# A two-layer transformer on one core: two conditioning loads moved to ScalarE's queue, and the cosine's angle put behind the first tile's scaling

## The chip, the cores and the metric

The kernel runs on one core of a Trainium2 chip. A core has five engines that run their own instruction streams and meet only at semaphores: TensorE (PE, matmuls and transposes), VectorE (DVE), ScalarE (ACT), GpSimd (POOL) and SyncE (SP, which here only issues transfers). Transfers between HBM and the on-chip memory are issued by SP's queue and ACT's queue and are carried by 16 DMA engines. The metric is the device time of one execution in microseconds (us). The kernel before takes 905.02 us, the median of 3 runs (904.16 to 906.2).

## The reference, cut to what matters

Two layers are applied to x (2048 tokens of 512 features, 32 sequences of 64), both conditioned on one vector per sequence. What matters here is the start of the first:

```python
def ada_rms(x, t, w, tw):
    n = x * jax.lax.rsqrt(jnp.mean(jnp.square(x), axis=-1, keepdims=True) + EPS)
    scale = t @ tw.T                                   # the conditioning
    return n * (w * (1.0 + scale))[:, None, :]
def apply_rope(x, pos_ids):
    ang = pos_ids.astype(jnp.float32)[:, :, None] * inv_freq
    cos, sin = ...                                     # of ang, twice beside each other
    x1, x2 = (x[..., :half], x[..., half:])
    return x * cos + jnp.concatenate([-x2, x1], axis=-1) * sin
h = ada_rms(x, time_emb, ln1_w, ln1_tw)                # layer 0
q, k, v = h @ Wq.T, h @ Wk.T, h @ Wv.T                 # 8 query heads, 1 key/value head of 64
q, k = apply_rope(q, pos_ids), apply_rope(k, pos_ids)
attn = softmax(q k^T / 8);  x = x + (attn v) @ Wo.T
h = ada_rms(x, time_emb, ln2_w, ln2_tw)
x = x + (silu(h @ Wg.T) * (h @ Wu.T)) @ Wd.T           # 2048 inner features
```

The second layer (a layernorm with scale and shift from the same conditioning vector, 16 query heads of 32, masked attention, an output projection, no MLP) follows; it lies far behind the change.

## The kernel before

The 2048 tokens are 16 tiles (t = 0 to 15) of 128 tokens, two sequences each. Layer 0's attention goes tile by tile in a loop over s (from -1 to 15), layer 1's in a loop over u. The MLP works on blocks of 512 tokens in 16 groups of 128 inner features and is cut into pieces; two tables (FILL0, FILL1) say how many pieces each engine does at which place of the loops. The first pieces come at s = 5. Large products are done as three fp32r matmuls of high and low parts, so every operand has a "high" cast on ACT and a "low" subtraction on DVE or POOL. The order of work on each engine is written out by hand, and every engine executes its stream strictly in that order; dependencies are semaphores.

The change lies before the loops. What happens there, by engine:

- **SP** issues `condt` (the conditioning vectors, transposed), then four slices of 256 KB of `ln1_twT` into `adaw0` (L261, k = 0 to 3), `xt` of tile 0 (L241), four slices of the joined query, key and value weights into `wst` (L264), `xres` and `xt` of the next tiles, and larger weights.
- **ACT** issues `posi` (the positions), `invt` (the inverse frequencies), `idn` (the identity for transposes) and the two halves of `lnw`; then it loads its table for the sine, copies the conditioning product out of PSUM (`condition_copy`), makes the rotary tables (`rope_tables`: four Sin activations into `cs0`, behind one wait on `ang_ready`), and then does the high casts of the weights (`split_qkv(0)` to `(3)`), the squares of tiles 0 and 1 and the high cast of tile 1 (`high_h(1)`).
- **PE** runs `keep_warm(4)` (matmuls whose result nobody reads), four `condition(k)` (the product of `condt` with slice k, each behind its own semaphore `ld_ln1[k]`) with a `keep_warm(1)` between, the transpose of the result, `keep_warm(3)`, and `first_qkv()` (tile 0 times the weights, in plain fp32, behind `a_hf`). Then come three warming matmuls, the conditioning of the second norm, two more warming matmuls, and the transposes of tile 0's rotated queries and keys (`qk_T(0)`, L557).
- **DVE** waits for `posi` and `invt`, and works the rotary angles: position times frequency, reduced to within pi (L922 to L943, result in `ex`), and pi/2 minus its absolute value (L947, L950, result in `t1`, the cosine's angle), whose last instruction signals `ang_ready`. Then `adaptive_scale(0)` (L957) makes the scale table, `scale_h(0)` (L998) applies it to tile 0 and signals `a_hf`; then `split_qkv(0)`, `scale_h(1)`, `mean_sq(0)`, `split_qkv(1)` and `(2)`, and `rope_mul(0)` (L1012 to L1014), which needs the tables.

`split_qkv(k)` on DVE waits for ACT's cast of the same slice, and `high_h(1)` on ACT waits for DVE's `scale_h(1)`, so the two engines pass work back and forth from `split_qkv(0)` until `rope_mul(0)`. `rope_mul(0)` is followed by the sum on POOL (L343, L344), `qk_T(0)` on PE, the copies, the scores and `qkv(1)` on PE, and so on round the loop.

Of the kernel before, what the change touches and what calls it, by code (L numbers as in the profile page):

```python
# [9 lines left out]
ALU = mybir.AluOpType  # L10
# [3 lines left out]
P = 128  # L14
# [15 lines left out]
def wait(eng, sem, count):  # L30
    if count > 0:
        eng.wait_ge(sem, count)
# [7 lines left out]
def build(nc, x, xT, pos, condT, ln1_w, ln1_twT, ln2_w, ln2_twT, WqkvT, WoT, gu, WdT,  # L40
          adaT, b_ada, Wq1T, Wkd, wkvuT, Wo1T, invf, rope1, ident, out):
    D = WoT.shape[0]
    KT = D // P
# [17 lines left out]
    with ExitStack() as ctx:  # L61
        def sb(name, shape, dt=F32, into=ctx):
            return into.enter_context(nc.sbuf_tensor(name, shape, dt))

        def sem(name):
            return ctx.enter_context(nc.semaphore(name))
# [24 lines left out]
        with ExitStack() as early:  # L91
# [4 lines left out]
            adaw0, adaw1 = sb("adaw0", [P, KT, D], into=early), sb("adaw1", [P, KT, D], into=early)  # L96
# [51 lines left out]
        ld_ln1 = [sem(f"ld_ln1_{m}") for m in range(KT)]  # L148
# [5 lines left out]
        ang_step, ang_ready, rope_tab = sem("ang_step"), sem("ang_ready"), sem("rope_tab")  # L154
# [25 lines left out]
        def by_entry(ap):  # L180
            return ap.rearrange("p k (b s) -> p k b s", b=2)

        def scale_of(tab, t):
            return tab[:, :, 2 * t:2 * t + 2].unsqueeze(3).broadcast_to([P, KT, 2, S])

        def in_layer(t):
            return 0 <= t < NT
# [44 lines left out]
        @block.sync  # L232
        def _(sp):
            xv = x.rearrange("(t p) d -> p t d", p=P)
            by_row = lambda w: w.rearrange("(k p) n -> p k n", p=P)

            def load_xT(t):
                if t == 2:
                    sp.wait_ge(a_qkv, 1)
                wait(sp, a_hl, t - 2)  # L240
                sp.dma_start(xt[t % 2][:, :, :], xT[t, :, :, :]).then_inc(ld_xt[t % 2], 16)  # L241

            def load_group(n):
                g, i = n % NG, n % 2
                wait(sp, m_gul, n - 1)
                sp.dma_start(rgu[i][:, :], gu[g, :, :]).then_inc(ld_gu[i], 16)
                wait(sp, m_wdl, n - 1)
                sp.dma_start(rwd[i][:, :], WdT[g * P:(g + 1) * P, :]).then_inc(ld_wd[i], 16)

            def store(t):  # L250
                sp.wait_ge(b_out, t + 1)
                sp.dma_start(out[t * P:(t + 1) * P, :], xres[:, t, :]).then_inc(b_st, 16)

            def store_last(h):
                sp.wait_ge(b_out, NT + h)
                cols = slice(D // 2 * h, D // 2 * (h + 1))
                sp.dma_start(out[(NT - 1) * P:NT * P, cols], xres[:, NT - 1, cols]).then_inc(b_st, 16)

            sp.dma_start(condt[:, :, :], by_row(condT)).then_inc(ld_cond, 16)
            for k in range(KT):  # L260
                sp.dma_start(adaw0[:, k, :], by_row(ln1_twT)[:, k, :]).then_inc(ld_ln1[k], 16)  # L261
            load_xT(0)
            for k in range(KT):
                sp.dma_start(wst[:, k, :], by_row(WqkvT)[:, k, :]).then_inc(ld_qkv[k], 16)  # L264
            sp.dma_start(xres[:, 0, :], xv[:, 0, :]).then_inc(ld_x0, 16)
            load_xT(1)
            sp.dma_start(xres[:, 1, :], xv[:, 1, :]).then_inc(ld_x1, 16)
            sp.dma_start(adaw1[:, :, :], by_row(ln2_twT)).then_inc(ld_ln2, 16)
            sp.dma_start(xres[:, 2, :], xv[:, 2, :]).then_inc(ld_x2, 16)
            sp.dma_start(wost[:, :, :], by_row(WoT)).then_inc(ld_wo, 16)  # L270
            load_xT(2)
            sp.dma_start(adaw2[:, :, :], by_row(adaT)).then_inc(ld_ada, 16)
            load_xT(3)
            sp.dma_start(xres[:, 3:6, :], xv[:, 3:6, :]).then_inc(ld_x3, 16)
            sp.dma_start(rope1t[:, :, :], rope1).then_inc(ld_rope1, 16)
            sp.dma_start(bada[:, :], b_ada).then_inc(ld_bada, 16)
            sp.dma_start(xres[:, 6:NT, :], xv[:, 6:NT, :]).then_inc(ld_x6, 16)
            load_xT(4)
            for n in range(2):
                load_group(n)  # L280
            sp.dma_start(w1st[:, :].rearrange("p (k n) -> p k n", k=KT), by_row(Wq1T)).then_inc(ld_w1, 16)
            done, n = 0, 2
            for s in range(HEAD - 2, NT):
                if in_layer(s + 3):
                    load_xT(s + 3)
                done += sum(FILL0.get(s, ()))
                while s >= HEAD and n < done // 4 + 3:
                    load_group(n)
                    n += 1
                if s == NT - 2:  # L290
                    sp.wait_ge(w1l, 1)
                    sp.dma_start(w1st[:, 0:D], Wkd).then_inc(ld_w1, 16)
                    sp.dma_start(w1st[:, D:D + 2 * P], wkvuT).then_inc(ld_w1, 16)
            sp.wait_ge(w1f, 1)
            sp.dma_start(w1st[:, :].rearrange("p (k n) -> p k n", k=KT), by_row(Wo1T)).then_inc(ld_w1, 16)
            for u in range(-1, NT + 1):
                done += sum(FILL1.get(u, ()))
                while n < min(done // 4 + 3, NN):
                    load_group(n)
                    n += 1  # L300
                if 0 < u < NT:
                    store(u - 1)
            for h in range(2):
                store_last(h)
            assert n == NN
            sp.wait_ge(b_st, 16 * (NT + 1))
# [612 lines left out]
        def _(dve):  # L919
# [5 lines left out]
            angle, turns, red = flat(t1), flat(t2), flat(ex)  # L925
# [8 lines left out]
            step = 4  # L934
            src = angle
            for part in (C1, C2, C3):
                dve.wait_ge(ang_step, step)
                dve.scalar_tensor_tensor(out=red, in0=turns, scalar=-part, in1=src, op0=ALU.mult,
                                         op1=ALU.add).then_inc(ang_step, 1)
# [3 lines left out]
            dve.tensor_scalar(red, red, float(np.float32(3.1415925)), -float(np.float32(3.1415925)),  # L943
                              ALU.min, ALU.max).then_inc(ang_step, 1)

            dve.wait_ge(ang_step, step + 1)
            dve.scalar_tensor_tensor(out=angle, in0=red, scalar=-1.0, in1=red, op0=ALU.mult,  # L947
                                     op1=ALU.max).then_inc(ang_step, 1)
            dve.wait_ge(ang_step, step + 2)
            dve.tensor_scalar(angle, angle, -1.0, float(np.pi / 2), ALU.mult, ALU.add).then_inc(ang_ready, 1)  # L950

            def adaptive_scale(n, tab, from_bank):
                if n == 0:
                    dve.wait_ge(ld_lnw, 32)
                dve.wait_ge(ada_T, n + 1)
                by_block = ps[:, from_bank, 0:P].rearrange("p (k b) -> p k b", k=KT)
                dve.scalar_tensor_tensor(out=tab[:, :, :], in0=by_block, scalar=1.0,  # L957
                                         in1=lnw[:, n, :].unsqueeze(2).broadcast_to([P, KT, NB]),
                                         op0=ALU.add, op1=ALU.mult).then_inc(ada_done, 1)
                dve.wait_ge(ada_done, n + 1)  # L960

            def split_qkv(k):
                dve.wait_ge(w0h, k + 1)
                dve.tensor_tensor(wql[:, k, 0:2 * QK0], wst[:, k, :], wqh[:, k, 0:2 * QK0],
                                  ALU.subtract).then_inc(w0l, 1)
# [29 lines left out]
            def scale_h(t):  # L995
                dve.wait_ge(ld_xt[t % 2], 16 * (t // 2 + 1))
                h = by_entry(xt[t % 2][:, :, :])
                dve.tensor_tensor(h, h, scale_of(sc_ln1, t), ALU.mult).then_inc(a_hf, 1)  # L998
# [221 lines left out]

            adaptive_scale(0, sc_ln1, BD[0])
            scale_h(0)
            split_qkv(0)
            scale_h(1)
            mean_sq(0)
# [112 lines left out]
        @block.scalar  # L1338
        def _(act):

            act.dma_start(posi[:, :], pos).then_inc(ld_pos, 16)
            act.dma_start(invt[:, :], invf).then_inc(ld_pos, 16)
            act.dma_start(idn[:, :], ident).then_inc(ld_idn, 16)
# [396 lines left out]
```

## Time and profile before

| | |
|---|---|
| median of 3 runs | 905.02 us (904.16 to 906.2) |
| the profiled execution's own time | 901.88 us |
| its span, first to last instruction | 900.1 us |
| mean granted TensorE clock | 0.998 |
| busy: PE | 878.1 us, 98% |
| busy: DVE, ACT, POOL | 569.8, 470.2, 414.8 us |
| moved by DMA | 73.19 MB, mean 81 GB/s |

The span is cut into 40 slices on the page, of 22.5 us each. PE is shown at 9 tenths or more in nearly all; the first slice has an 8, and its DMA engines stand at 9 tenths with 343 GB/s. Everything the change touches lies within the first 20 us. Times in the rows are microseconds from the start of the span; a time in square brackets is how long the engine was idle before the row and which instruction ended that idleness ("issue" where the profile shows no other cause). "ACTq" and "SPq" are the sequencers that issue transfers.

### The profile page before, as it was taken

How to read it: one execution, taken by the hardware profiler on the slowest of the kernel's cores; microseconds unless marked ns; L12 is line 12 of the kernel's file. 1: busy time of each engine (PE TensorE's matmuls, PEld its weight loads, DVE VectorE, ACT ScalarE, POOL GpSimd, SP SyncE). 2: the span in 40 equal slices, each digit the busy share in tenths (PEclk: the TensorE clock that was granted, in tenths of full speed). 3: DMA queues.
4: the chain of work that ended last, by engine and by line, in shares of the span. 5: the costliest groups of instructions: out<-in, count | busy, mean ns of one | idle time of the engine just before them, and what ended most of it. 6: DMA issues, size and time to landing. Idle time of an engine off the chain costs nothing.

```text
span 900.1 us, 16086 instructions
## 1 busy us (share of the span) xinstructions
PE 878.1 (98%) x6190; PEld 736.7 (82%) x6190; DVE 569.8 (63%) x943; ACT 470.2 (52%) x862; POOL 414.8 (46%) x315
## 2 busy tenths in 40 slices
PE   8898999999999999999999999999999999998997
PEld 5787888888888888887887888888888888888885
DVE  5775556556556556567456676585774765757886
ACT  5666446455445445445537556455464464444662
POOL 3566545445435445446447545453444344431331
PEclk9999999999999999999999999999999999999999
DMA  9901222122222221122132222221222222100001
GB/s 343 333 24 40 103 81 82 71 82 83 71 83 83 71 82 72 71 71 88 71 117 71 71 71 83 71 83 52 68 83 71 83 83 71 69 3 13 25 25 36
DMA packets 31003, 73.19 MB, mean 81 GB/s; under 512 B 4304, under 2 KB 4816, under 8 KB 30928
## 3 DMA queue, kind: packets, MB, share of 16 engines
q1 hardware_dynamic: 30208, 72.07, 23.0%
q8 instruction: 50, 0.82, 0.4%
q10 hardware_dynamic: 720, 0.09, 0.1%
q14 instruction: 25, 0.20, 0.1%
HBM read 67.96 MB, written 4.19 MB: 80 GB/s over the span
## 4 chain that ended last, share of the span: by engine, by line
PE 83%; issue 6%; DVE 5%; POOL 4%; ACT 2%; DMA 0%; POOLq 0%; ACTq 0%; DVEq 0%
PE ps L484 25%; PE ps L486 24%; PE ps L485 24%; PE ps L763 2%; PE ps L590 1%; PE ps L572 1%; PE ps L741 1%; PE ps L751 1%; PE ps L557 1%; POOL qr L343 1%; PE ps L717 1%; POOL qr L395 1%; PE ps L690 1%; POOL stat L317 1%; POOL kr L394 1%
## 5 line engine op out<-in xcount | busy, mean ns | idle before, releaser
L360 POOL TENSOR_TENSOR gul<-rgu,guh 128x1024 fp32r<-128x1024 f32 x64 | 156.4, 2444 | 187.8 <-ACT guh L1453 187.8
L1067 DVE TENSOR_TENSOR xres<-ps,xres 128x512 f32<-128x512 f32 x256 | 174.6, 687 | 88.2 <-PE ps L486 88.2
L484 PE MATMUL ps<-h2h,guh 128*128 128x512 f32 x512 | 205.8, 402 | 0.7 <-issue 0.7
L486 PE MATMUL ps<-h2l,guh 128*128 128x512 f32 x512 | 199.7, 390 | 0.0
L485 PE MATMUL ps<-h2h,gul 128*128 128x512 f32 x512 | 199.5, 390 | 0.0
L486 PEld LDWEIGHTS ps<-h2l,guh 128*128 128x128 f32 x512 | 96.1, 188 | 20.8
L484 PEld LDWEIGHTS ps<-h2h,guh 128*128 128x128 f32 x512 | 96.2, 188 | 20.3 <-issue 1.1
L485 PEld LDWEIGHTS ps<-h2h,gul 128*128 128x128 f32 x512 | 96.3, 188 | 18.7
L484 PE MATMUL ps<-wdh,ah 128*128 128x512 f32 x256 | 101.0, 394 | 1.2 <-DVE al L1062 1.2
L1475 ACT CAST ah<-af 128x512 fp32r<-128x512 f32 x64 | 39.7, 621 | 119.2 <-DVE af L1080 119.2
L486 PE MATMUL ps<-wdl,ah 128*128 128x512 f32 x256 | 99.8, 390 | 0.0
L485 PE MATMUL ps<-wdh,al 128*128 128x512 f32 x256 | 99.7, 390 | 0.0
L1080 DVE TENSOR_TENSOR af<-ps,sg 128x512 f32<-128x512 f32 x64 | 44.2, 690 | 82.9 <-PE ps L486 71.5
L365 POOL TENSOR_TENSOR wdl<-rwd,wdh 128x512 fp32r<-128x512 f32 x64 | 82.0, 1282 | 28.1 <-ACT wdh L1461 28.1
L1467 ACT ACTIVATE sg<-ps 128x512 f32<-128x512 f32 x64 | 38.3, 598 | 74.7 <-PE ps L486 74.4
L1453 ACT CAST guh<-rgu 128x1024 fp32r<-128x1024 f32 x64 | 67.0, 1046 | 0.0
L1062 DVE TENSOR_TENSOR al<-af,ah 128x512 fp32r<-128x512 f32 x64 | 56.0, 875 | 11.0 <-ACT ah L1475 7.4
L484 PEld LDWEIGHTS ps<-wdh,ah 128*128 128x128 f32 x256 | 48.0, 188 | 14.9 <-DVE al L1062 5.1
L317 POOL TENSOR_TENSOR stat<-stat,minus_half 128x1 f32<-128x1 f32 x48 | 37.7, 785 | 44.7 <-DVE stat L987 29.5
L486 PEld LDWEIGHTS ps<-wdl,ah 128*128 128x128 f32 x256 | 48.0, 188 | 10.1
L485 PEld LDWEIGHTS ps<-wdh,al 128*128 128x128 f32 x256 | 48.1, 188 | 9.3
L343 POOL TENSOR_TENSOR qr<-t 128x576 f32<-128x576 f32 x16 | 23.4, 1460 | 50.2 <-DVE t L1014 50.2
(172 smaller groups left out, 1688.7 us busy)
## 6 DMA issues: line engine op xcount, KB each, us to landing
rgu<-gu SPq DMA_DIRECT2D x64, 512.0 KB, 3.6
rwd<-WdT SPq DMA_DIRECT2D x64, 256.0 KB, 2.7
xt<-xT SPq DMA_DIRECT2D x16, 256.0 KB, 3.1
out<-xres SPq DMA_DIRECT2D x15, 256.0 KB, 2.3
xres<-x SPq DMA_DIRECT2D x1, 2560.0 KB, 16.2
adaw<-adaT SPq DMA_DIRECT2D x1, 2048.0 KB, 10.3
wst<-WqkvT SPq DMA_DIRECT2D x4, 320.0 KB, 6.0
adaw<-ln_twT SPq DMA_DIRECT2D x4, 256.0 KB, 4.2
```

Of the source, the lines that this page charges most:

```text
L317: pool.tensor_tensor(col, col, minus_half[:, :], ALU.pow).then_inc(signal, 1)
L360: pool.tensor_tensor(gul[i][:, :], rgu[i][:, :], guh[i][:, :], ALU.subtract).then_inc(m_gul, 1)
L365: pool.tensor_tensor(wdl[i][:, :], rwd[i][:, :], wdh[i][:, :], ALU.subtract).then_inc(m_wdl, 1)
L484: pe.matmul(dst, lh, rh, start=start, stop=False)
L485: pe.matmul(dst, ll, rh, start=False, stop=False)
L486: return pe.matmul(dst, lh, rl, start=False, stop=stop)
L1062: dve.tensor_tensor(al[n % 2][:, :], af[:, :], ah[n % 2][:, :], ALU.subtract).then_inc(m_al, 1)
L1067: dve.tensor_tensor(at, bank(BD[i % 2]), at, ALU.add).then_inc(m_x, 1)
L1080: dve.tensor_tensor(af[:, :], bank(BU), sg[:, :], ALU.mult).then_inc(m_af, 1)
L1453: act.copy(guh[i][:, :], rgu[i][:, :]).then_inc(m_guh, 1)
L1467: act.activation(sg[:, :], bank(BG), ACT.Silu).then_inc(m_sg, 1)
L1475: act.copy(ah[n % 2][:, :], af[:, :]).then_inc(m_ah, 1)
```

## The change

Two edits, and nothing else in the program moves. First, slices 1 and 3 of `adaw0` are issued by ACT's queue, ahead of its five small transfers; SP's loop keeps slices 0 and 2. Second, the two DVE instructions for the cosine's angle, with their waits and the signal `ang_ready`, become a function `cosine_angle()` that is called behind `scale_h(0)` and ahead of `split_qkv(0)`.

```diff
@@ -257,7 +257,7 @@
             sp.dma_start(condt[:, :, :], by_row(condT)).then_inc(ld_cond, 16)
-            for k in range(KT):
+            for k in range(0, KT, 2):
                 sp.dma_start(adaw0[:, k, :], by_row(ln1_twT)[:, k, :]).then_inc(ld_ln1[k], 16)
             load_xT(0)
@@ -943,11 +943,12 @@
-            dve.wait_ge(ang_step, step + 1)
-            dve.scalar_tensor_tensor(out=angle, in0=red, scalar=-1.0, in1=red, op0=ALU.mult,
-                                     op1=ALU.max).then_inc(ang_step, 1)
-            dve.wait_ge(ang_step, step + 2)
-            dve.tensor_scalar(angle, angle, -1.0, float(np.pi / 2), ALU.mult, ALU.add).then_inc(ang_ready, 1)
+            def cosine_angle():
+                dve.wait_ge(ang_step, step + 1)
+                dve.scalar_tensor_tensor(out=angle, in0=red, scalar=-1.0, in1=red, op0=ALU.mult,
+                                         op1=ALU.max).then_inc(ang_step, 1)
+                dve.wait_ge(ang_step, step + 2)
+                dve.tensor_scalar(angle, angle, -1.0, float(np.pi / 2), ALU.mult, ALU.add).then_inc(ang_ready, 1)
@@ -1220,6 +1221,7 @@
             adaptive_scale(0, sc_ln1, BD[0])
             scale_h(0)
+            cosine_angle()
             split_qkv(0)
@@ -1338,6 +1340,9 @@
+            for k in range(1, KT, 2):
+                act.dma_start(adaw0[:, k, :], ln1_twT.rearrange("(k p) n -> p k n", p=P)[:, k, :]
+                              ).then_inc(ld_ln1[k], 16)
             act.dma_start(posi[:, :], pos).then_inc(ld_pos, 16)
```

How the instructions stand is shown in three pieces. Line numbers behind the edits are one to five higher in the changed file. VectorE before, from the reduction of the angle (L943) over the cosine's angle (t<-ex, t<-t) to the first low part of the weights (wql):

```order
L943 TENSOR_SCALAR ex<-ex 128x512
L947 SCALAR_TENSOR_TENSOR t<-ex 128x512
L950 TENSOR_SCALAR t<-t 128x512
L957 SCALAR_TENSOR_TENSOR sc_ln<-ps,lnw 128x128
L998 TENSOR_TENSOR xt<-xt,sc_ln 128x512
L964 TENSOR_TENSOR wql<-wst,wqh 128x640
```

and VectorE in the same place after the change:

```order
L943 TENSOR_SCALAR ex<-ex 128x512
L958 SCALAR_TENSOR_TENSOR sc_ln<-ps,lnw 128x128
L999 TENSOR_TENSOR xt<-xt,sc_ln 128x512
L948 SCALAR_TENSOR_TENSOR t<-ex 128x512
L951 TENSOR_SCALAR t<-t 128x512
L965 TENSOR_TENSOR wql<-wst,wqh 128x640
```

The scale table and tile 0's scaling have moved ahead of the cosine's angle; the low part of the weights stays behind both. ScalarE at the start of the program, before, where the four `cs` rows are the sines:

```order
L1341 DMA posi<-pos 128x16
L1342 DMA invt<-invf 128x32
L1343 DMA idn<-ident 128x128
L1344 DMA lnw<-ln_w 128x4
L1345 DMA lnw<-ln_w 128x4
L1582 ACT_TABLE_LOAD
L1582 ACTIVATE spare<-minus_half 128x1
L1354 COPY cnd<-ps 128x128
L1361 ACTIVATE cs<-ex 128x16x32
```

and after the change:

```order
L1344 DMA adaw<-ln_twT 128x512 x2
L1346 DMA posi<-pos 128x16
L1347 DMA invt<-invf 128x32
L1348 DMA idn<-ident 128x128
L1349 DMA lnw<-ln_w 128x4
L1350 DMA lnw<-ln_w 128x4
L1587 ACT_TABLE_LOAD
L1587 ACTIVATE spare<-minus_half 128x1
L1359 COPY cnd<-ps 128x128
L1366 ACTIVATE cs<-ex 128x16x32
```

Two issues stand ahead of everything else; the order behind them is as it was, and all four sines still come ahead of the casts. On SyncE the four issues of L261 have become two:

```order
 L259 DMA condt<-condT 128x4x32
-L261 DMA adaw<-ln_twT 128x512 x4
+L261 DMA adaw<-ln_twT 128x512 x2
 L241 DMA xt<-xT 128x512
 L264 DMA wst<-WqkvT 128x640 x4
```

Every later issue of SP stands two places earlier.

## Rows read from the trace of the kernel before

**Rows 1.** The chain of waits up to 70 us: start, length, piece.

```profile
by line: issue 18.9%; POOL qr L343 10.9%; POOL stat L317 6.9%; PE ps L557 4.7%; DMA invt<-invf 4.0%; DVE smx L1035 4.0%; DVE ex L1038 4.0%; PE ps L590 3.8%; POOL qr L344 3.5%; PE ps L484 3.3%; DVE ex L938 3.0%; PE ps L485 3.0%; PE ps L486 3
...
1.18 2.80 DMA invt<-invf
4.01 0.19 DVE posf L922
...
9.70 0.63 ACT cs L1361
...
16.25 0.81 DVE t L1012
```

**Rows 2.** Timeline of ScalarE: start, length, instruction, idle before it.

```profile
0.73 0.42 ACTq L1341 DMA_DIRECT2D posi<-pos  x1
...
8.99 0.27 ACT L1354 COPY cnd<-ps 128x128 f32<-128x128 f32 x1 [4.38 <-PE ps L493]
...
11.79 0.71 ACT L1349 CAST wqh<-wst 128x640 fp32r<-128x640 f32 x1
```

**Rows 3.** Timeline of VectorE.

```profile
8.05 0.43 DVE L943 TENSOR_SCALAR ex<-ex 128x512 f32<-128x512 f32 x1
8.51 0.69 DVE L947 SCALAR_TENSOR_TENSOR t<-ex 128x512 f32<-128x512 f32 x1
9.23 0.43 DVE L950 TENSOR_SCALAR t<-t 128x512 f32<-128x512 f32 x1
9.81 0.29 DVE L957 SCALAR_TENSOR_TENSOR sc_ln<-ps,lnw 128x128 f32<-128x128 f32 x1
10.13 0.69 DVE L998 TENSOR_TENSOR xt<-xt,sc_ln 128x512 f32<-128x512 f32 x1
```

**Rows 4.** Timeline of TensorE's matmuls.

```profile
1.34 3.78 PE L526 MATMUL ps<-bdv 128*128 128x256 f32 x8 [1.34 <-POOL minus_half L313]
...
10.88 4.57 PE L535 MATMUL ps<-wst,xt 128*128 128x320 f32 x16
...
17.69 1.13 PE L526 MATMUL ps<-bdv 128*128 128x256 f32 x4
20.24 0.65 PE L557 MATMUL ps<-idn,qr 128*128 128x128 f32 x4 [1.42 <-POOL qr L344]
...
21.68 0.69 PE L572 MATMUL ps<-kT,qT 64*64 64x64 f32 x32 [0.68 <-ACT qT L1407]
```

**Rows 5.** Transfers on ACT's queue: size each, median us from issue to landing.

```profile
idn<-ident ACTq DMA_DIRECT2D x1, 64.0 KB, 3.5
lnw<-ln_w ACTq DMA_DIRECT2D x2, 2.0 KB, 4.0
...
invt<-invf ACTq DMA_DIRECT2D x1, 16.0 KB, 2.8
```

**Rows 6.** The same for SP's issue at 1.23 us (slice 0).

```profile
adaw<-ln_twT SPq DMA_DIRECT2D x1, 256.0 KB, 3.8
```

**Rows 7.** The same for SP's issue of slice 3, the last before 3.19 us.

```profile
adaw<-ln_twT SPq DMA_DIRECT2D x1, 256.0 KB, 4.7
```

**Rows 8.** The same for SP's issue at 5.87 us (x of tile 0).

```profile
xres<-x SPq DMA_DIRECT2D x1, 256.0 KB, 6.6
```

**Rows 9.** Page, part 1: busy time, share, instructions.

```profile
PE 878.1 (98%) x6190; PEld 736.7 (82%) x6190; DVE 569.8 (63%) x943; ACT 470.2 (52%) x862; POOL 414.8 (46%) x315
```

**Rows 10.** Stretches: length, busy PE, PEld, DVE, ACT, POOL, granted clock, DMA share, GB/s.

```profile
28.80:30.50 1.70, 0.00 (x0) 0.00 (x0) 1.70 (x2) 1.62 (x5) 1.70 (x3) 1.00 1.05 386
```

**Rows 11.** The same stretches near the end of the program.

```profile
824.00:826.00 2.00, 2.00 (x37) 1.83 (x37) 0.29 (x1) 0.58 (x1) 1.17 (x1) 0.83 0.36 135
826.00:828.00 2.00, 2.00 (x70) 1.77 (x67) 1.16 (x2) 1.30 (x2) 0.00 (x0) 0.50 0.03 8
828.00:830.00 2.00, 2.00 (x12) 2.00 (x11) 1.96 (x3) 0.57 (x1) 0.00 (x0) 0.82 0.00 0
```

**Rows 12.** Timeline of TensorE ahead of those stretches.

```profile
824.00 0.66 PE L717 MATMUL ps<-idn,qr 128*128 128x128 f32 x4 [2.03 <-POOL qr L395]
```

## The prediction

> **What bounds the kernel now.** Over the whole span PE is busy 98% [rows 9], and the MLP pieces that fill it begin at s = 5. Whatever delays PE before that is paid in full, because the stream behind has no slack to swallow it. So I read the start: first the chain of waits, then the three compute engines' timelines over the same microseconds, then the transfers, from issue to landing.
>
> The chain does not begin with the conditioning. It begins with `invt`, the inverse frequencies on ACT's queue, which land at 4.0 us; DVE has waited for them from the start [rows 1]. DVE's angle work fills 4.01 to 9.66, ACT starts the sines at 9.70 [rows 1, 3], four of them take it to 11.79, where the first cast of the weights starts [rows 2]; casts on ACT and subtractions on DVE then alternate until `rope_mul(0)` at 16.25 [rows 1]. From there the chain runs over POOL's sum, `qk_T(0)` at 20.24, the scores at 21.68 [rows 4], `qkv(1)` behind them and round the loop. In the chain up to 70 us the only transfer among the pieces named is `invt` [rows 1]. So what sets the pace is when the sines start. `first_qkv` does not: it ends at 15.45 (10.88 plus 4.57) [rows 4], 0.80 us before `rope_mul(0)` starts.
>
> The conditioning's loads don't bound either. Slice 0 is issued at 1.23 us and lands 3.8 us later, at 5.03 [rows 6]; PE is in its first warming matmuls until 5.12 (1.34 plus 3.78) [rows 4]. Slice 3 is issued at about 2.7 us and lands 4.7 later, at about 7.4 [rows 7], and the product's copy starts at 8.99 [rows 2].
>
> **The change part by part.** All sums are differences to the profiled execution (901.88 us, span 900.1). Its 1.8 us outside the span are not touched, so a difference found here is added to the median of the runs, 905.02.
>
> *Slices 1 and 3 earlier.* They come 1 us or more sooner, but PE does the four products in its order, slice 0 first, which is issued at the time it was, and behind warming matmuls that end at 5.12 anyway. I cost the gain at nothing: what hides it is PE's own stream. If the sharing of the DMA engines held slice 0 back by some tenths, the product would be late by as much; by the next step DVE isn't ready for it sooner.
>
> *`posi` and `invt` later.* Two issues stand ahead of them. An issue takes 0.42 us plus the gap, `posi` at 0.73 and `invt` at 1.18 being 0.45 to 0.48 apart [rows 1, 2], so `invt` is issued at about 2.13 instead of 1.18. For issue to landing the trace has 2.8 us for `invt` with little ahead of it, and 3.5 and 4.0 for `idn` and the mean of `lnw`, which travelled beside SP's large slices [rows 5]. With 2.8 it lands at 4.93, with 4.0 at 6.1. Ahead of it on its queue there are now 512 KB, where there were 8 KB; slice 3 on SP's queue, with 832 KB ahead of it, took 4.7 [rows 7], which would make 6.8. I take 5.8, nearest to the tiny transfers under load: DVE starts 1.8 us later than at 4.01.
>
> The Trainium skill (DMA: Bandwidth & Descriptors, Queues, rings and completion order) says that SP and ACT each own one row of rings on the same 16 engines, that an engine consumes one ring in order and takes turns between rows. By that `posi` and `invt` have to follow both slices, and the landing lies at the late rather than the early end. The same page (Issuing engines are not separate DMA queues) says that issuing from a second queue saves only issue time; that speaks against the load half of the change. No row of before shows small transfers behind large ones on one queue.
>
> *The cosine's angle behind the scaling.* From the landing, DVE takes 4.50 us to the point where L947 stood (4.01 to 8.51) [rows 1, 3]. There now stands `adaptive_scale(0)`. It also needs the transposed product, as before at 9.81. With 5.8 DVE is there at 10.30, so DVE itself decides. Then 0.32 for the table (9.81 to 10.13) and 0.72 for the scaling (0.69 and a gap of 0.03 as between L947 and L950), then the cosine's angle: 0.72 + 0.43 + 0.04 until ACT starts = 1.19 (8.51 to 9.70) [rows 1, 3]. The sines start at 10.30 + 0.32 + 0.72 + 1.19 = 12.53, where it was 9.70: **2.83 us later**. `ang_ready` is one signal behind the cosine's angle, so the two sines that need only the reduced angle wait too. Even with `invt` where it was, DVE would reach the scale table early and stand at 9.81, and the sum is 9.81 + 0.32 + 0.72 + 1.19 = 12.04, 2.34 late. That is the low end, whatever the queue does down to a landing at 5.3. With a landing at 6.8 the high end is 3.83.
>
> Queued behind the sines on ACT are all casts, and behind them `split_qkv(0)` on DVE, `scale_h(1)`, `high_h(1)` and so on: the whole alternation of 4.46 us (11.79 to 16.25) keeps its inner order and shifts by 2.83. x of tile 0, which lands at 12.5 (5.87 plus 6.6) [rows 8], comes 1 us earlier and was needed at about 12.5, now at 15.3: nothing is late there. `first_qkv` starts at about 11.4, 0.5 later than 10.88, and ends at 15.9: still ahead of `rope_mul(0)`, now at 19.1. ACT's table load comes 1 us later, within its idle 4.38 us ahead of 8.99 [rows 2]; `lnw` was landing at about 6.8 and would be at about 9 now, before DVE needs it at 10.3.
>
> *A wait that grows behind it.* PE's warming matmuls ended at 18.82 (17.69 plus 1.13), then it was idle 1.42 us until 20.24 [rows 4]. After the change the warming ends near 19.3 and `qk_T(0)` comes at 23.07: 3.8 us idle. Late in this execution PE was idle 2.03 us [rows 12], and in the stretches behind it the granted clock was 0.83, 0.50 and 0.82, that is between 2.4 and 1.2 GHz [rows 11]; the missing clock adds up to 2 x (0.17 + 0.50 + 0.18) = 1.7 us. With 1.7 us idle at 28.8 the clock stayed 1.00 [rows 10]. The new gap is longer than the one that was followed by the drop. If the drop comes, it falls on the tile's transposes, the scores and `qkv(1)`, all on the chain, with one idle 0.68 us between [rows 4] (0.35 of clock not needed): 1.35 us. Bounds: nothing, and 3.4, if the clock falls twice.
>
> Sum of the likeliest: 2.83 + 1.35 = 4.2, so 905.02 + 4.2 = **909.2 us**.
>
> **The rivals.**
>
> *A, the clock holds.* The same delay of the sines without a drop: 905.02 + 2.8 = 907.8. For it: five transposes lie between two idle stretches, and the early gap of 1.42 did nothing. Against: the gap is nearly three times that.
>
> *B, the queue is worse than I take it.* `invt` at 6.8 and a drop: 3.83 + 1.7, 910.6.
>
> *C, the delay is given back.* The late drop of the clock near 825 us [rows 11] lies behind 2 us of idleness that is not much longer than gaps that cost nothing. If a shift of the whole stream by 3 us makes it stay away, 1.7 comes back, and with the clock held at the start it is 905.02 + 2.8 - 1.7 = 906.1, within the noise. For it: only that the drop is single. Against: nothing in the change touches that place.
>
> *D, faster.* SP's loads behind slice 2 are issued 0.97 us earlier, and tile 0 is scaled ahead of the cosine's angle. If `posi` and `invt` passed the slices, and if PE's `first_qkv` or x of tile 0 set `rope_mul(0)` rather than the sines, the whole start would move up by up to that 0.97: 904.05. The point from which it decides is the start of the sines: at or before 9.70. For it: x of tile 0 lands at the very moment its square starts [rows 8]. Against: the sum above, whose low end puts the sines at 12.04 without any help of the queue. That the change simply doesn't do what it says is in part of every case here: slices 1 and 3 come sooner, and nobody was waiting.
>
> **How the numbers follow.** A measurement of this kernel tells about 0.2%, 1.8 us, from no change. Forecast 0.45, A 0.30, B 0.10, C 0.11, D 0.04. The forecast, A and B are slower by more than 0.2% (above 906.8): 0.85 with a little of A lost to the noise, counted 0.84. Same: C and what A loses, 0.12. Faster: D, 0.04. The range goes from 906.7 (A with `invt` at its early end, 907.4, less some of the runs' spread, which was 1 us either way) to 911.0 (B and that spread).
>
> **What would show it.** DVE's first instruction moves from 4.01 to 5 to 6.8. The scale table stands ahead of the cosine's angle and starts at 9.8 to 11.3. The first sine starts at 12.0 to 13.5, the first cast at 14.1 to 15.6, `rope_mul(0)` at 18.6 to 20.1, each 4.46 behind the one before as now. `first_qkv` starts within 0.9 us of 10.88. PE's idle time ahead of L557 (some lines further down) grows from 1.42 to 3 us and more, and the stretch from 22 to 28 us has a granted clock below 1 if the drop is there. From the first MLP piece on, everything is the same, later by the sum. I am wrong if the sines start before 11.5, if they are late and `rope_mul(0)` isn't, or if the delay at the first MLP piece is much smaller than at `rope_mul(0)`.

## The result, and the profile after

The changed kernel takes 909.87 us (median of 5 runs, 908.8 to 910.99) and the kernel before 905.02 (5 runs, 903.69 to 906.2). The ratio is 1.0062, 95% interval 1.0039 to 1.0086: slower, beyond what the measurement leaves open. The profiled execution took 908.8 us with a span of 907.0 and a mean granted clock of 0.994. Among the runs of the experiments below, one execution each of `e1_loads`, `e3_warm` and `e5_gap` was disturbed (3061.64, 1091.57 and 2464.0 us) and is left out of the medians.

VectorE after the change, the rows that answer to [rows 3] and to the start of the chain in [rows 1]:

```profile
7.30 0.18 DVE L922 CAST posf<-posi 128x16 f32<-128x16 int32 x1 [7.30 <-DMA invt<-invf]
...
11.34 0.43 DVE L943 TENSOR_SCALAR ex<-ex 128x512 f32<-128x512 f32 x1
11.68 0.28 DVE L958 SCALAR_TENSOR_TENSOR sc_ln<-ps,lnw 128x128 f32<-128x128 f32 x1
12.00 0.69 DVE L999 TENSOR_TENSOR xt<-xt,sc_ln 128x512 f32<-128x512 f32 x1
12.61 0.69 DVE L948 SCALAR_TENSOR_TENSOR t<-ex 128x512 f32<-128x512 f32 x1
13.33 0.43 DVE L951 TENSOR_SCALAR t<-t 128x512 f32<-128x512 f32 x1
...
20.35 0.81 DVE L1013 TENSOR_TENSOR t<-ps,cs 128x640 f32<-128x640 f32 x1
```

DVE starts 3.3 us later than at 4.01, still waiting for `invt`. The table and the scaling follow the reduction at once, without a wait for PE, and the cosine's angle ends at 13.76. ScalarE, to be held against 9.70 and 11.79 in [rows 1, 2]:

```profile
8.79 0.27 ACT L1359 COPY cnd<-ps 128x128 f32<-128x128 f32 x1 [3.10 <-PE ps L493]
13.79 0.63 ACT L1366 ACTIVATE cs<-ex 128x512 f32<-128x512 f32 x1 [4.74 <-DVE t L951]
...
15.89 0.71 ACT L1354 CAST wqh<-wst 128x640 fp32r<-128x640 f32 x1
```

ACT now stands idle 4.74 us ahead of its sines. Everything behind is 4.10 us late: the sines, the first cast and `rope_mul(0)` (20.35 to 16.25). TensorE, to be held against [rows 4]:

```profile
5.34 0.43 PE L493 MATMUL ps<-adaw,condt 128*32 128x128 f32 x8 [0.21 <-DMA adaw<-ln_twT]
...
12.75 4.58 PE L535 MATMUL ps<-wst,xt 128*128 128x320 f32 x16 [1.95 <-DVE xt L999]
...
24.34 0.65 PE L557 MATMUL ps<-idn,qr 128*128 128x128 f32 x4 [3.65 <-POOL qr L344]
```

The product waits 0.21 us for slice 0, which it did not before. The idle time ahead of `qk_T(0)` has grown from 1.42 to 3.65 us. The landings, as in [rows 5, 6]:

```profile
adaw<-ln_twT SPq DMA_DIRECT2D x1, 256.0 KB, 4.0
posi<-pos ACTq DMA_DIRECT2D x1, 8.0 KB, 4.4
invt<-invf ACTq DMA_DIRECT2D x1, 16.0 KB, 5.0
```

`invt` is issued at 2.26 and takes 5.0 us instead of 2.8. Last, stretches behind the gap (columns as in rows 10; the granted clock is the third figure from the end):

```profile
26.00:28.00 2.00, 2.00 (x36) 1.88 (x33) 1.02 (x2) 1.84 (x4) 0.00 (x0) 0.50 1.03 378
28.00:30.00 2.00, 2.00 (x11) 2.00 (x11) 1.91 (x5) 0.63 (x1) 1.32 (x2) 0.69 0.99 294
```

The clock is at its low level of 1.2 GHz in the first of them, at 2.4 GHz again by 30. The fifth tile's transposes, before and then changed:

```profile
60.60 0.66 PE ps L557 x4
66.18 0.66 PE ps L557 x4
```

The delay is 4.10 us at the first tile and 5.58 at the fifth. At the first transposes of layer 1 (799.96 against 794.37) it is still 5.59: nothing is given back in 730 us of filled PE. At the end of the program two things happen that no row links to the start. Before, the clock fell behind the transposes at 824.00 [rows 11, 12]; in the changed kernel it did not, behind the same 2.03 us of idleness, and 1.30 us come back by the next tile. The tile behind it before, then the two tiles in the changed kernel:

```profile
836.84 0.66 PE L717 MATMUL ps<-idn,qr 128*128 128x128 f32 x4 [0.29 <-POOL qr L395]
829.57 0.66 PE L717 MATMUL ps<-idn,qr 128*128 128x128 f32 x4 [2.03 <-POOL qr L395]
841.11 0.66 PE L717 MATMUL ps<-idn,qr 128*128 128x128 f32 x4 [0.31 <-POOL qr L395]
```

The delay, 5.57 at the first of these tiles, is 4.27 at the second. In the last 15 us the changed kernel's profiled execution had a long stretch of low clock, which that of before did not have, and 2.6 us are added: 6.9 us of span in all.

### The profile page after: what moved, and what is told of

It is laid out like the page before. It is cut to its first block, busy times and chain, and to the rows that moved or that the text cites. A ratio compares the mean times of both kernels' runs of the same rounds, so it can differ in the third digit from the quotient of the medians.

```text
span 907.0 us, 16086 instructions
## 1 busy us (share of the span) xinstructions
PE 880.5 (97%) x6190; PEld 739.2 (82%) x6190; DVE 569.2 (63%) x943; ACT 470.1 (52%) x862; POOL 415.1 (46%) x315
## 4 chain that ended last, share of the span: by engine, by line
PE 82%; issue 6%; DVE 5%; POOL 4%; ACT 2%; DMA 1%; POOLq 0%; ACTq 0%; DVEq 0%
PE ps L484 25%; PE ps L486 24%; PE ps L485 24%; PE ps L763 2%; PE ps L590 1%; PE ps L572 1%; PE ps L751 1%; PE ps L557 1%; POOL qr L343 1%; PE ps L717 1%; POOL qr L395 1%; PE ps L741 1%; PE ps L690 1%; POOL stat L317 1%; POOL kr L394 1%
```

## The experiments

The points of comparison are two: when the sines and the first tile's transposes start (the delay), and how long it is from the first tile's transposes to the fifth's, 40.3 to 40.4 us at full clock (before: 20.24 to 60.60). "Gap" is PE's idle time ahead of `qk_T(0)`. The kernel before, run beside them, had medians of 904.46 us (beside `e1` to `e4`), 904.34 (`e5` to `e8`), 904.45 (`e9` to `e11`) and 905.23 (`e12`).

**The loads alone** (`e1_loads`).

```diff
-            for k in range(KT):
+            for k in range(0, KT, 2):
                 sp.dma_start(adaw0[:, k, :], ...)
+            for k in range(1, KT, 2):
+                act.dma_start(adaw0[:, k, :], ...)      # ahead of posi; the cosine's angle stays
```

> Loads only; the cosine's angle stays ahead of the scale table. My theory (the small transfers land late behind the slices, the angle chain sets the sines): DVE starts at 7.3 as in the changed kernel, sines 3.3 us later than before at 13.0, rope_mul(0) at 19.5. Tile 0 is scaled only at 14.1, so PE stands idle about 3.2 us ahead of first_qkv and only 1.4 us ahead of qk_T(0); the clock may fall in the first of these gaps instead. +3.3 us without a drop, +4 to +5 with it. Rival (the loads are harmless, the moved cosine does it all): sines at 9.7 and no change.

906.02 us, ratio 1.0019 (1.0005 to 1.0032). Its VectorE, and then its TensorE:

```profile
7.55 0.17 DVE L922 CAST posf<-posi 128x16 f32<-128x16 int32 x1 [7.55 <-DMA invt<-invf]
...
20.21 0.82 DVE L1012 TENSOR_TENSOR t<-ps,cs 128x640 f32<-128x640 f32 x1 [0.35 <-PE ps L535]
```

```profile
14.17 6.00 PE L535 MATMUL ps<-wst,xt 128*128 128x320 f32 x16 [2.76 <-DVE xt L998]
...
24.22 0.66 PE L557 MATMUL ps<-idn,qr 128*128 128x128 f32 x4 [0.68 <-POOL qr L344]
```

The sines start at 13.23, 3.5 late. As expected, PE is idle ahead of `first_qkv` instead, the clock falls there (0.50 in the stretch from 14 to 16) and the product takes 6.00 instead of 4.57 us; it even becomes the bound of `rope_mul(0)`, which waits 0.35 us for it. Behind it the gap is small and 40.35 us pass to the fifth tile. "The loads are harmless" has fallen. In the runs this kernel is only 1.6 us above before, less than the 4 us by which its first transposes are late. Its mean granted clock over the runs is a little higher (0.9962 against 0.9956 of the kernel before beside it), which accounts for a small part of that; the rest stays open.

**The cosine's angle alone** (`e2_cosine`).

```diff
             scale_h(0)
+            cosine_angle()      # all loads as before
             split_qkv(0)
```

> Cosine's angle behind the scaling only; all loads as before. My theory: DVE starts at 4.0, scale table at 9.8 as before because the transposed product decides, sines at 12.0 (+2.3), first_qkv at 10.9 unchanged, PE idle 3.7 us ahead of qk_T(0) and a drop of the clock worth 1.5 us: +3.8 in all at the second tile. Rival (only the queue matters): no change. Rival (the drop needs more than this gap): +2.3.

907.55 us, ratio 1.0031 (1.0020 to 1.0043). The scale table starts at 9.85; the sines and the transposes stand here:

```profile
11.95 0.63 ACT L1363 ACTIVATE cs<-ex 128x512 f32<-128x512 f32 x1 [2.73 <-DVE t L951]
```

```profile
22.50 0.91 PE L557 MATMUL ps<-idn,qr 128*128 128x128 f32 x4 [3.65 <-POOL qr L344]
```

The delay is 2.25 us, as worked out for any landing up to 5.3: `invt` landed at 5.47 in this execution, and it made no difference. The gap is 3.65, the clock falls twice (0.50 between 24 and 28 us, 0.54 between 38 and 40), and it is 44.15 us to the fifth tile, 3.8 more; I had expected one drop worth 1.5. So each edit is slower alone. They don't add up (3.5 and 2.3 against 4.1 together), since the wait of one covers part of the other's.

**The two small loads first on ACT's queue** (`e4_small_first`).

```diff
             act.dma_start(posi[:, :], pos).then_inc(ld_pos, 16)
             act.dma_start(invt[:, :], invf).then_inc(ld_pos, 16)
+            for k in range(1, KT, 2):                   # was ahead of posi
+                act.dma_start(adaw0[:, k, :], ...)
```

> The changed kernel with posi and invt issued ahead of slices 1 and 3 on ACT's queue. My theory (order in the queue makes invt late): DVE starts at 4.0 to 4.3, sines at 12.0 (+2.3), the clock drops in a gap of 3.7 us, +3.8 at the second tile: the same as the cosine alone. Rival (two slices on a second queue slow all transfers, whatever the order): invt lands after 5.5 and the sines start after 12.3.

908.83 us, ratio 1.0048 (1.0031 to 1.0065). VectorE:

```profile
5.01 0.18 DVE L922 CAST posf<-posi 128x16 f32<-128x16 int32 x1 [5.01 <-DMA invt<-invf]
...
10.81 0.29 DVE L958 SCALAR_TENSOR_TENSOR sc_ln<-ps,lnw 128x128 f32<-128x128 f32 x1 [1.34 <-DMA lnw<-ln_w]
```

`invt` is 2.3 us earlier than in the changed kernel, so the order on the queue made most of its lateness; at 5.01 it is still later than the 4.0 to 4.3 I had expected, and within what the loads of before gave (3.8 to 5.5). But `lnw` comes behind the slices, as in the changed kernel, where DVE is too late to notice; here DVE waits 1.34 us for it, and the sines start at 12.93, not at 12.0 as I had expected. I had moved the wait, not removed it. The gap was 3.65 and the way to the fifth tile 44.07 us.

**More warming behind the change** (`e3_warm`), and **less warming in the kernel before** (`e5_gap`).

```diff
# e3_warm, the changed kernel            # e5_gap, the kernel before
                 if s == -1:
-                    keep_warm(2)        # e5_gap also drops keep_warm(3) behind first_qkv
+                    keep_warm(8)        # e5_gap: no call at all
```

> The changed kernel with 8 instead of 2 warming matmuls ahead of qk_T(0); 6 x 0.46 us fill 2.7 of its 3.65 us of idleness. My theory: rope_mul(0) stays 4.1 us late, the granted clock stays 1.00 up to 40 us, and the second tile's transposes are 4.1 late instead of 5.6; the time falls by 1.5 us against the changed kernel, to +4.1 less or plus what the late clock does. Rival (the 1.5 us come from something else, such as DMA): 5.6 late as in the changed kernel.

> The kernel before, without the five warming matmuls between first_qkv and qk_T(0) (3 and 2 of them; nobody reads their result). Nothing else waits on them, so the sines and rope_mul(0) stay where the landing of invt puts them, and PE is idle about 3.7 us ahead of qk_T(0). My theory (the gap alone brings the clock down): a granted clock of about 0.5 behind it and the second tile's transposes 1.5 to 2.7 us later behind the first's than the 10.3 us of before. Rival (the drop in the changed kernel came of something else): 10.3 us between the two as before.

The warmed kernel took 907.64 us, ratio 1.0049 (1.0028 to 1.0069), 3.2 us above before instead of 4.85; the intervals overlap, so the runs don't settle that. Its trace does: gap 1.06, 40.35 us to the fifth tile, the clock at 1.00 up to 40 us, and a delay of 4.58 at the first tile that is 4.57 at the fifth. In the other direction the kernel without warming took 907.10 us, ratio 1.0020 (1.0004 to 1.0036), with a gap of 4.01 and 41.71 us to the fifth tile. Its profiled execution is the one of 2464.0 us: the clock stood at 0.16 from about 550 us on, for a reason that no row shows, so only its start is read here. The transposes of the one and the other:

```profile
24.82 0.66 PE L557 MATMUL ps<-idn,qr 128*128 128x128 f32 x4 [1.06 <-POOL qr L344]
```

```profile
20.90 0.66 PE L557 MATMUL ps<-idn,qr 128*128 128x128 f32 x4 [4.01 <-POOL qr L344]
```

The warmed kernel showed a second thing that I had not expected, at the start. TensorE and VectorE:

```profile
5.57 0.66 PE L493 MATMUL ps<-adaw,condt 128*32 128x128 f32 x8 [0.44 <-DMA adaw<-ln_twT]
6.15 1.22 PE L526 MATMUL ps<-bdv 128*128 128x256 f32 x2
7.30 0.66 PE L493 MATMUL ps<-adaw,condt 128*32 128x128 f32 x8
```

```profile
12.15 0.29 DVE L958 SCALAR_TENSOR_TENSOR sc_ln<-ps,lnw 128x128 f32<-128x128 f32 x1 [0.82 <-PE ps L503]
```

A product and a warming matmul take 1.74 us together where they took 0.98: PE runs at half pace, after 0.44 us without work ahead of them, until 10.8. So the transposed product comes more than 2 us late and DVE, late as it is, waits 0.82 us more for it. Half pace is how PE starts in every execution: the eight instructions of the first warming took 3.78 us [rows 4] and 3.7 to 3.8 in all the others, and eight of the same size took 1.99 us at 18 us in `e12_before_warm`. What differs is when it ends.

**Both kernels again** (`e6_before_again`, `e9_before_3`, `e8_after_again`, `e10_after_3`), unchanged.

> The kernel before, unchanged, profiled once more. The cosine's-angle kernel had the loads of before and yet invt landed at 5.47, not at 4.01. If the landing differs from execution to execution, it is not at 4.01 here but anywhere from 4 to 5.5, and the sines move with it one to one; if the 1.4 us came of the edit, it is at 4.0 again.

> The changed kernel, unchanged, profiled once more, for the spread of its own start: with the landing of invt between 6.9 and 7.6, as in the three kernels so far that had both slices ahead of it, sines at 13.4 to 14.1, the clock again down behind the gap. If the landing is a matter of chance as a whole, it could come as early as 5.5.

> The kernel before, a third profile. Of two so far one had the clock at its full level throughout the first 40 us and one had it fall near 21 us and again near 32 us, though PE was idle only 1.65 us ahead of it. Theory (the drop is also common in the kernel before, so most of it is no part of the difference): a drop within the first 40 us here too, span near 905. Rival (it was an exception): clock 1.00 up to 40 us, span near 900.

> The changed kernel, a third profile. invt at 6.8 to 7.6, sines at 13.3 to 14.1, a drop of the clock within 24 to 30 us as in the two others. What is left of the difference to the kernel before, when both have a drop, is the sines' delay, 3.6 to 4.1 us.

They took 907.46, 903.23, 911.3 and 909.93 us. In `e8_after_again` `invt` was a shade earlier than I had expected (6.83 against 6.9 to 7.6). Beside the first profiled execution of each kernel:

```text
                          before                 changed
DVE starts (invt)      4.01  3.98  4.05       7.30  6.83  7.10
sines start            9.70  9.67  9.73      13.79 13.31 14.30
gap                    1.42  1.65  0.93       3.65  3.65  3.64
first transposes      20.24 20.21 20.28      24.34 23.85 24.85
fifth transposes      60.60 63.43 60.61      66.18 67.12 68.78
```

Two things follow. The kernel before is not free of the drop: in the second execution it fell behind a gap of 1.65, and a second time ahead of the second tile's transposes. In the third, where my expectation had called for a drop again, the clock stayed at 1.00 up to 65 us. And the mean difference is 4.10 us at the first tile and 5.81 at the fifth, so the clock adds 1.7. In the third execution of the changed kernel PE waited 0.76 us for slice 0 and again ran at half pace:

```profile
5.88 0.66 PE L493 MATMUL ps<-adaw,condt 128*32 128x128 f32 x8 [0.76 <-DMA adaw<-ln_twT]
```

There the scale table waited 0.63 us for the product, and the sines came at 14.30, past the 14.1 that I had expected at the latest. Whether the wait causes the half pace isn't shown: in `e9_before_3`, `e4_small_first` and `e11_start2` the first product and its warming ran at half pace too, without any wait ahead of them.

**Two versions with an earlier start** (`e7_start`, `e11_start2`), both from the kernel before.

```diff
-                act.wait_ge(ang_ready, 1)               # both kernels
+                act.wait_ge(ang_step, 8)                # the reduced angle alone
                 (two sines of ex)
+                act.wait_ge(ang_ready, 1)
                 (two sines of the cosine's angle)
# e7_start: rope_mul(0) ahead of split_qkv(2) on DVE, rope_sum(0) ahead of low_h(1) on POOL
# e11_start2: SP issues xres of tile 0 behind xt of tile 0, xt of tile 1 behind two slices of wst
```

> The kernel before with three moves that follow from the chain: ACT's first two sines wait only for the reduced angle, not for the cosine's; DVE does rope_mul(0) ahead of split_qkv(2); POOL does the sum for tile 0 ahead of low_h(1). My theory (the sines' start sets the start of the program): with invt at 4.0 the first sine starts at 9.3 behind the copy of the conditioning product, 0.4 earlier, and rope_mul(0) at 15.5, 0.7 earlier, where first_qkv holds it; with a later invt the gain is larger, up to 1.2. Faster by about 0.8 us, which the runs can hardly tell from nothing. Rival (POOL or the weights' low parts become the bound): no gain at the second tile's transposes.

> The kernel before with two edits: ACT's first two sines wait only for the reduced angle, and SP issues x of tile 0 ahead of the weights' slices and xt of tile 1 behind the second of them. My theory (behind the sines the next limit was x of tile 0, landing at 12.5, then first_qkv): first sine at about 8.7, square(0) at 11.5 instead of 12.5, rope_mul(0) at 15.3, 0.9 us earlier, and the first tile's transposes 0.9 earlier at 19.3; about 0.9 us faster in the runs, the edge of what they tell. Rival (the later slices of the weights become late): first_qkv ends after 15.5 and nothing is gained.

`e7_start` took 904.63 us, ratio 0.9991 (0.9972 to 1.0011): no difference. Its sines start at 8.63, a whole microsecond earlier, and that is lost twice, on ScalarE and on GpSimd:

```profile
12.50 0.63 ACT L1383 ACTIVATE sq<-xres 128x512 f32<-128x512 f32 x1 [1.03 <-DMA xres<-x]
```

```profile
19.27 0.90 POOL L344 TENSOR_TENSOR qr<-t 128x64 f32<-128x64 f32 x1
```

The next limit is x of tile 0 [rows 8], and the small sum on POOL took 0.90 us instead of 0.32 beside DVE's `split_qkv(3)`, which itself took 1.96 instead of 0.81.

`e11_start2` is faster than both: 902.3 us, ratio 0.9967 (0.9953 to 0.9980). Its profiled execution doesn't show my reason: the conditioning ran at half pace at first and slice 3 was late, the sines started at 9.81, `rope_mul(0)` at 16.37, and the first transposes at

```profile
20.36 0.66 PE L558 MATMUL ps<-idn,qr 128*128 128x128 f32 x4 [0.73 <-POOL qr L345]
```

No start earlier by 0.9, but a gap of 0.73 and a mean granted clock of 0.997 over the 12 executions, against 0.995 of the kernel before. But the profiled execution, 903.33 us, was among the slowest of the 12, and the clock is not all. Executions with the same mean clock can be held against each other:

```text
mean clock     before (78, beside the experiments)   changed (7)    e11_start2 (12)
0.990          908.15 (3)                            910.99 (1)
0.991          908.46 (6)                            911.30 (1)
0.992          906.24 (3)                            909.87 (4)
0.994          905.55 (22)                           908.80 (1)     904.17 (1)
0.996          904.21 (31)                                          903.15 (5)
0.998          902.94 (12)                                          901.47 (4)
1.000          901.08 (1)                                           900.42 (2)
```

The entries are mean times in us, the number of executions in brackets. At equal clock `e11_start2` is still 0.7 to 1.5 us faster. So a start earlier by about the 0.9 that I had expected is likely in the executions that were not profiled; it isn't shown in any trace. `e7_start` is 0.5 us below before at 0.996 (903.73).

**The gap by itself** (`e12_before_warm`).

```diff
                 if s == -1:
-                    keep_warm(2)        # the kernel before
+                    keep_warm(4)
```

> The kernel before with 4 instead of 2 warming matmuls ahead of qk_T(0), nothing else. In the 13 profiles so far the clock fell behind qk_T(0) in all 8 in which PE was idle 1.63 us or longer ahead of it (one of three of the kernel before, with 1.65), and in none of the 5 with 1.42 us or less. Two more matmuls take 0.9 us out of the gap, 1.4 to 1.7 before. My theory (the length of this gap decides): 0.5 to 0.8 us of gap, clock 1.00 up to 60 us, 40.3 us from the first to the fifth tile's transposes, and in the runs a mean clock near 0.997 instead of 0.995 and 1 to 1.5 us less time. Rival (the drop is chance, and the faster start version gained by its loads): no difference to the kernel before.

903.21 us against 905.23, ratio 0.9985 (0.9969 to 1.0002), mean clock 0.9973 against 0.9952 over 12 and 17 executions. The interval just touches no change. The profiled execution had a gap of 0.98 (I had expected 0.5 to 0.8), 40.35 us to the fifth tile and a mean clock of 1.000 at a span of 899.8, although its first transposes were 0.8 us later than before, because x of tile 0 landed later (ScalarE waited 0.45 us for it, and the first cast and `rope_mul(0)` are 5.00 us apart instead of 4.46):

```profile
21.01 0.66 PE L557 MATMUL ps<-idn,qr 128*128 128x128 f32 x4 [0.98 <-POOL qr L344]
```

All 14 profiled executions together: with a gap of 1.63 us or more the clock fell behind `qk_T(0)` in 8 of 8 and the way to the fifth tile was 41.7 to 44.2 us; with 1.42 or less in 0 of 6, and it was 40.3 to 40.4. A drop seldom stays alone: ahead of the second tile's transposes PE is idle 2.05 to 2.06 us in those 8, and the clock fell again in 6 of them. That makes two sizes: the way to the fifth tile was 1.3 to 1.5 us longer with one drop and 2.9 to 3.8 with two. But the gap's length alone does not decide. In the 6 executions in which the clock held behind `qk_T(0)`, PE was idle longer ahead of the second tile than ahead of the first, and the clock stayed at 1.00, as here before:

```profile
30.56 0.66 PE L557 MATMUL ps<-idn,qr 128*128 128x128 f32 x4 [1.78 <-POOL qr L344]
```

And near 825 us the same 2.03 us were followed by a drop before and by none in the changed kernel. What else counts stays open. At equal mean clock `e12_before_warm` is within 0.3 us of before from 0.994 to 0.998 (905.47, 904.50, 902.99), so its 2.0 us go with the clock. For `e11_start2`, by an estimate from the same table, about 1 us is left at equal clock and the rest goes with the clock.

## Why the prediction was right, point by point

*What bounds the start.* Right. In 11 of the 14 profiled executions `rope_mul(0)` follows the first cast by 4.46 to 4.47 us (15.89 to 20.35 here, as 11.79 to 16.25 before), and the delay stands unchanged 730 us later. The other three show what is close behind: PE's product in `e1_loads` (4.89), x of tile 0 in `e12_before_warm` (5.00), and the changed order in `e7_start` (4.94). The first cast itself follows the first sine by 2.1 us; "each 4.46 behind the one before" in the prediction is right for `rope_mul(0)` alone.

*Slices 1 and 3 earlier are worth nothing.* Right in the main: the copy starts at 8.79 instead of 8.99 and DVE isn't there until 11.68. The sentence that a late slice 0 would make the product late by as much was wrong. In `e3_warm` 0.44 us of waiting and in `e10_after_3` 0.76 us went with a conditioning at half pace and a product more than 2 us late, and DVE had to wait for it.

*The landing of `invt`.* The term that was mis-sized. I took 5.8 and bounded it by 6.8; it landed at 7.30, 6.83 and 7.10. I chose by the tiny transfers beside large slices [rows 5], but the right neighbour was the transfer with large ones ahead of it [rows 7], and even that was low: with 4.7 from issue the high end was 6.8, and all three landed beyond it. So every time that I had given for the start was missed at its late end: the sines at 13.79 against 12.0 to 13.5, `rope_mul(0)` at 20.35 against 20.1 at the latest, `first_qkv` 1.87 us late instead of within 0.9. The Trainium skill (DMA: Bandwidth & Descriptors, Queues, rings and completion order) says that each engine takes a queue's descriptors in ring order; the trace agrees: with `posi` and `invt` ahead of the slices DVE started at 5.01, behind them at 7.30, and the landings from issue were 3.8 and 5.0 us; the other 1.1 us between the two starts are the later issue.

*The steps on DVE.* Right to a tenth or two: from its start to the sines 6.49 us against 6.73 worked out. The low end, 2.34, was measured alone as 2.25. The sum, 2.83, was 4.10 in the mean of three; the landing, 7.08 in the mean against 5.8, makes all of the difference.

*The clock.* Gap 3.65 us against the 3.8 forecast, the drop came, and it cost 1.5 us in the profiled execution against my 1.35 and up to 3.6 in another. What I left out is that the kernel before pays it too in some executions, in one of three profiled. The difference that counts is 1.7. I argued from the length of a gap alone, and that is too little: 1.65 us was followed by a drop and 1.78 by none in one and the same kernel. For a gap of 3.65 us it made no difference.

*The rivals.* A, the clock holds: in none of five profiled executions with this gap of 3.65 us (the changed kernel's three, `e2_cosine` and `e4_small_first`). B had the queue right. C, the delay given back near 825 us: the drop there was indeed missing in the changed kernel's profile and gave back 1.30 us (I had priced it at 1.7), and the low clock at the end took 2.6. In the other executions of both kernels the drop near 825 to 838 us came in `e6_before_again`, `e8_after_again` and `e10_after_3` and not in `e9_before_3`: it comes and goes in both. D, faster: its point, the sines at or before 9.70, was passed by 3.6 us and more.

*The sum.* 4.2 forecast, 4.85 measured; over all 7 executions of the changed kernel and the 83 of before that ran beside the kernels it is 5.3 (909.9 against 904.6). In the traces the delay was 1.3 us larger than forecast and the clock term 0.3 larger, 5.8 together, and the medians show less, so the nearness of 4.2 to 4.85 is in part luck. An estimate from the table of mean clocks: at equal clock the changed kernel is 2.8 to 3.6 us slower, and the rest, about 2 us, goes with its lower mean clock (0.992 against 0.995). One reason why the 4.10 of the traces is more than that may be that the three profiled executions of before were early ones: with the same loads, `invt` landed at 4.03 to 5.47 in the four other kernels' traces. That isn't shown for the runs.

## What to carry to other kernels

Before a transfer goes ahead of others on a queue, look who waits for those others: here two large slices that nobody waited for pushed back two small ones that the whole start hangs on. When an engine has one signal for several results, moving the last of them moves them all. And a delay of a few microseconds in a start with little PE work is not only itself: look what PE's idle time becomes, because two more warming matmuls went with 2.0 us less, about as much as the changes of order in `e11_start2`, though the interval for the two matmuls just touches no change.

## What the runs showed of the hardware that I had not expected

- Ahead of the first tile's transposes the edge of the clock's drop is narrow: behind 1.42 us of idleness or less it fell in 0 of 6 executions, behind 1.63 or more in 8 of 8. It is no rule for another place: ten microseconds later 1.77 to 1.78 us were followed by no drop in 6 of 6. One drop cost 1.3 to 1.5 us, two cost 2.9 to 3.8.
- The start of the program varies between executions of one and the same code: a product and its warming matmul took 1.74 or 0.98 us, for the first one or up to three of them, while the granted clock of the stretch read 1.00. PE ran at half pace until somewhere between 5 and 11 us. With ACT's loads as before, `invt` landed between 3.8 and 5.5 us.
- A second queue doesn't leave the first one alone: with the slices at the head of ACT's queue `condt`, on SP's, took 3.1 to 3.4 us to land instead of 2.0 to 2.4. With two small transfers ahead of the slices (`e4_small_first`) it took 2.2.
- In one place of `e7_start` a DVE subtraction of 128x640 and a small POOL addition took 1.96 and 0.90 us instead of 0.81 and 0.32. The subtraction began at 18.03, behind the start of POOL's large sum (17.39 to 19.30), and ended 0.69 after it. Before, it began at 17.84, 0.09 ahead of that sum, and took 0.81, while the sum took 1.97.
